# A hand-ordered two-way Mamba scan on one core: scalings of turned states, copies and output products moved in the queues of ScalarE and TensorE

## What is computed

```python
# x: 32 sequences x 256 tokens x 128 channels, fp32
x = x + 0.5 * moe(layernorm(x))                       # 8 experts, 2 per token, hidden 512
x = x + mamba(layernorm(x), w1) + mamba(flip(layernorm(x)), w2)
x = x + 0.5 * moe(layernorm(x))

# mamba: 256 inner channels, 16 states n, depthwise convolution of 4 taps
xi, z = split(x @ in_w.T);  xc = silu(conv(xi) + conv_b)
dt, B, C = split(xc @ xp_w.T);  delta = softplus(dt @ dtp_w.T + dtp_b)
h[n] = h[n] * exp(delta * A[n]) + (delta * xc) * B[n]   # a scan over the 256 tokens
y = sum_n h[n] * C[n] + xc * D;  out = (y * silu(z)) @ out_w.T
```

## Time and profile before

| | before |
|---|---|
| median of 3 runs | 3043.69 us (3041.62 to 3048.03) |
| the profiled execution's own time | 3050.79 us |
| its span | 3048.9 us |
| the Mamba layer's scans, first to last | 653.29 to 2395.38 us |
| busy share: TensorE / VectorE / ScalarE / GpSimd | 84% / 77% / 59% / 74% |

### The profile page before, as it was taken

One profiled execution on the slowest core, in us unless ns is written; L12 is line 12 of the kernel. 1 busy time (PEld: TensorE's weight loads), 2 busy tenths in 40 slices (PEclk: granted clock), 3 DMA queues, 4 the chain that ended last, 5 costly groups with the idle time before them and its releaser, 6 DMA issues.

```text
span 3048.9 us, 41641 instructions
## 1 busy us (share of the span) xinstructions
PE 2546.1 (84%) x12256; PEld 1705.2 (56%) x12256; DVE 2360.4 (77%) x3613; ACT 1809.3 (59%) x3320; POOL 2263.1 (74%) x1360
## 2 busy tenths in 40 slices
PE   4788888868999889989999998998998767888883
PEld 2777778734444444544444444454444457777773
DVE  6755545589999999999999999999998784555556
ACT  3344444457777777777777778777777424444441
POOL 1566656549989899998998989999899535666662
PEclk8899999989999999999999999999999988999997
DMA  6011111143333333333333333333333401111115
GB/s 213 16 40 40 39 38 39 37 155 106 102 94 94 98 95 101 102 94 98 99 98 100 98 97 96 99 102 94 99 99 100 161 12 38 39 39 40 38 40 181
DMA packets 159520, 257.04 MB, mean 84 GB/s; under 512 B 22130, under 2 KB 64018, under 8 KB 158610
## 3 DMA queue, kind: packets, MB, share of 16 engines
q1 hardware_dynamic: 140482, 211.31, 23.4%
q0 software_dynamic: 18464, 37.79, 4.6%
q10 hardware_dynamic: 432, 6.29, 0.5%
HBM read 221.75 MB, written 33.55 MB: 84 GB/s over the span
## 4 chain that ended last, share of the span: by engine, by line
PE 49%; issue 17%; ACT 17%; DVE 10%; POOL 5%; DMA 1%; another core or an unknown queue 1%; SPq 0%; ACTq 0%; POOLq 0%; DVEq 0%
PE bank L1280 14%; PE bank L1446 13%; PE bank L1301 9%; ACT scaled L1142 4%; ACT over L1109 4%; DVE buf L859 4%; POOL buf L493 2%; PE bank L1261 2%; PE bank L1435 2%; POOL buf L506 2%; DVE bank L831 2%; PE bank L1386 2%; DVE X L753 2%; PE bank L1357 2%; ACT bank L1053 1%
## 5 line engine op out<-in xcount | busy, mean ns | idle before, releaser
L506 POOL TENSOR_TENSOR buf<-buf 128x1024 f32<-128x1024 f32 x512 | 1200.8, 2364 | 152.8 <-DVE buf L859 139.4
L1446 PE MATMUL bank<-buf,id_sb 128*128 128x512 f32 x2048 | 977.8, 609 | 46.9 <-ACT bank L1053 39.1
L859 DVE TENSOR_TENSOR_SCAN buf<-over,bank 128x512 f32<-128x512 f32 x768 | 888.2, 1203 | 26.4 <-PE bank L1435 26.4
L1446 PEld LDWEIGHTS bank<-buf,id_sb 128*128 128x128 f32 x2048 | 375.7, 195 | 430.0 <-issue 334.3
L1280 PE MATMUL bank<-parts 128*128 128x256 f32 x3456 | 529.7, 300 | 72.3 <-issue 71.5
L1109 ACT ACTIVATE over<-wgu,negA 128x510 f32<-128x510 f32 x768 | 505.3, 710 | 56.5 <-DVE buf L859 52.7
L455 POOL DMA_INDIRECT token_outputs<-buf,slot_out x288 | 299.1, 1038 | 297.8 <-ACT buf L1004 226.8
L1280 PEld LDWEIGHTS bank<-parts 128*128 128x128 f32 x3456 | 462.8, 200 | 92.3 <-issue 89.5
L725 DVE TENSOR_TENSOR buf<-buf,bank 128x512 f32<-128x512 f32 x288 | 196.8, 684 | 352.1 <-ACT buf L998 205.8
L831 DVE TENSOR_TENSOR bank<-wgu,bank 128x512 f32<-128x512 f32 x512 | 326.9, 684 | 94.8 <-PE bank L1401 62.8
L1301 PE MATMUL bank<-buf 128*128 128x128 f32 x2304 | 307.4, 290 | 92.6 <-issue 67.9
(11 more groups left out here) (166 smaller groups left out, 2839.5 us busy)
## 6 DMA issues: line engine op xcount, KB each, us to landing
buf<-state_rows SPq DMA_DIRECT2D x640, 256.0 KB, 3.3
token_rows<-buf SPq DMA_DIRECT2D x32, 256.0 KB, 2.3
wd_sb<-token_outputs SPq DMA_DIRECT2D x16, 512.0 KB, 4.3
buf<-token_outputs SPq DMA_DIRECT2D x16, 512.0 KB, 5.0
buf<-token_rows,slot_token POOLq DMA_INDIRECT x288
token_outputs<-buf,slot_out POOLq DMA_INDIRECT x288
out<-X SPq DMA_DIRECT2D x16, 256.0 KB, 3.7
wgu<-wgT ACTq DMA_DIRECT2D x1, 2048.0 KB, 8.5
```

Source lines behind the costliest of these rows:

```text
L506: pool.tensor_tensor(hC[:, b, :].rearrange("p (c w) -> p c w", c=C), hs[:, b, :].rearrange("p (c w) -> p c w", c=C), Cs[:, b, :].unsqueeze ...
L859: V.tensor_tensor_scan(hs[:, b, w], dA[:, b, c, :, :].rearrange("p s t -> p (s t)"), source, 0.0, ALU.mult, ALU.add).then_inc(s[f"scan_don ...
L1446: ins = M.matmul(bank[4 + c], id_sb[:, :], hC[:, n % R, c * W:(c + 1) * W], start=False, stop=(n == NS - 1), skip_group_check=True)
```

## The change

- ScalarE scales the turned states 8, 11 and 14 earlier: 8 inside `silus` in state 4 (before: state 6), 11 in state 6 (before: 9), 14 in state 9 (before: 12). State 3 is scaled in state 1 as before.
- ScalarE copies the two halves of duT in states 0 and 1 of the turn (before: state 15 of the turn before, and state 0). In state 9 it copies the columns of B behind the scaling, and the residual copy goes from state 8 to 9, ahead of the scaling.
- TensorE turns the second half of du at the end of its work in state 0; the output product is cut in two halves, in states 7 and 8 (before: whole in 7); and `spread` is issued at another place of the loop.

```diff
-ACT_AT = {"duT0": 15, "duT1": 0, ..., "silus": 4, "xnT": 6, "hi": 7, "res": 8, "BT": 9, ...}
+ACT_AT = {"duT0": 0, "duT1": 1, ..., "silus": 4, "xnT": 6, "hi": 7, "res": 9, "BT": 9, ...}
-SCALE_AT = {1: 3, 6: 8, 9: 11, 12: 14}
+SCALE_AT = {1: 3, 6: 11, 9: 14}
...
-def spread_lead(n):
-    return 1 if on_pool(n - 1) else 2
...
 def silus(p, r, between):            # ScalarE
     for c in range(C):
         act.wait_ge(s["pe_pre"], done(PE_PRE, f"conv{c}_{r}", p))
         step(A.activation(xc[r][:, c * W:(c + 1) * W], bank[6 + c], ACT.Silu, ...))
+    between()                        # scale_by_B of state 8
...
 # ScalarE, in state n
+                        if n == ACT_AT["duT0"]:
+                            copy_duT(p * 2 + r, 0)
                         if n == ACT_AT["duT1"]:
                             copy_duT(p * 2 + r, 1)
...
+                        if n == ACT_AT["res"] and not (first and r == 0):
+                            residual(p * 2 + r - 1, p - 1 if r == 0 else p)
                         if n in SCALE_AT:
                             scale_by_B(p * 2 + r, SCALE_AT[n])
+                        if prep and n == ACT_AT["BT"]:
+                            columns_of_B(2 * pv + rv)
...
 # TensorE, in state n
                         if on_turn(n + 1):
                             turn_back(p, r, n + 1)
-                        for m in (n + 1, n + 2):
-                            if not on_pool(m) and not on_turn(m) and m - spread_lead(m) == n:
-                                ... spread m
+                        m = n + 2
+                        if m < NS and not on_pool(m) and not on_turn(m) and not on_turn(n):
+                            spread(p, r, m)
+                        elif m >= NS and prep and not on_turn(n):
+                            spread(pv, rv, m - NS)
...
-                        if n == PE_AT["duT1"]:      # ahead of the sum and the convolution
-                            turn_du(u, r, 1)
...
+                        if n == PE_AT["duT1"]:      # behind them
+                            turn_du(u, r, 1)
...
-                        if n == PE_AT["out"] and not (first and r == 0):
-                            project_out(u - 1, 1 - r, ...)
+                        if n in (PE_AT["out"], PE_AT["out"] + 1) and not (first and r == 0):
+                            project_out(u - 1, 1 - r, n - PE_AT["out"], ...)
...
+                        if on_turn(n):              # at the end of the state
+                            if n + 2 < NS:
+                                spread(p, r, n + 2)
+                            elif prep:
+                                spread(pv, rv, n + 2 - NS)
```

More of the change, by code:

```diff
@@ L44 @@
 POOL_AT = {"rstd": 0, "du": 12}
-ACT_AT = {"duT0": 15, "duT1": 0, "xn": 2, "skip": 3, "silus": 4, "xnT": 6, "hi": 7, "res": 8, "BT": 9, "parts": 10, "ln": 11}
+ACT_AT = {"duT0": 0, "duT1": 1, "xn": 2, "skip": 3, "silus": 4, "xnT": 6, "hi": 7, "res": 9, "BT": 9, "parts": 10, "ln": 11}
 PE_AT = {"duT1": 0, "z": 4, "xt": 5, "xdbl": 6, "out": 7, "dt": 9, "BT": 9, "duT0": 15}
@@ L816, in gate @@
                 dve.wait_ge(s["y_done"], (u + 1) * NS)
-                wait(dve, s["pe_post"], u)
+                wait(dve, s["pe_post"], 2 * u)
                 for c in range(C):
@@ L1063, in normT, with silus @@
                 A.activation(xnT[:, 1, :, ::-1], src, ACT.Copy).then_inc(s["act_norm"], 1)
-            def silus(p, r):
+            def silus(p, r, between):
                 for c in range(C):
@@ L1097, in residual @@
             def residual(u, p):
-                act.wait_ge(s["pe_post"], u + 1)
+                act.wait_ge(s["pe_post"], 2 * u + 2)
                 A.activation(X[:, p * G:(p + 1) * G, :], bank[7].rearrange("p (t d) -> p t d", t=G),
@@ L1156, in pair @@
                             skip(p * 2 + r, r)
+                        if not prep and n == ACT_AT["silus"]:
+                            scale_by_B(p * 2 + r, TURNED_UNITS[1])
                         if prep and n == ACT_AT["silus"]:
-                            silus(pv, rv)
-                        if prep and n == ACT_AT["BT"]:
-                            columns_of_B(2 * pv + rv)
+                            silus(pv, rv, lambda: scale_by_B(p * 2 + r, TURNED_UNITS[1]))
                         if r == 0 and not last and n == ACT_AT["xnT"]:
@@ L1167, in pair @@
                             decay(pv, rv, n + DECAY_LEAD - NS)
+                        if n == ACT_AT["res"] and not (first and r == 0):
+                            residual(p * 2 + r - 1, p - 1 if r == 0 else p)
                         if n in SCALE_AT:
                             scale_by_B(p * 2 + r, SCALE_AT[n])
-                        if n == ACT_AT["res"] and not (first and r == 0):
-                            residual(p * 2 + r - 1, p - 1 if r == 0 else p)
+                        if prep and n == ACT_AT["BT"]:
+                            columns_of_B(2 * pv + rv)
                         if not prep:
@@ L1186, in _ @@
             normT(0)
-            silus(0, 0)
+            silus(0, 0, lambda: None)
             split_hi(0, 0)
@@ L1193, in _ @@
                 decay(0, 0, n)
-            copy_duT(0, 0)
             pair(0, True, False)
@@ L1377, in project_dt, with project_out @@
                     ins.then_inc(s["pe_pre"], 1)
-            def project_out(u, r, after):
+            def project_out(u, r, half, after):
                 pe.wait_ge(s["gated"], u + 1)
@@ L1383, in project_out @@
                 after()
-                for t in range(G):
+                for t in (2 * half, 2 * half + 1):
                     for c in range(C):
@@ L1490, in pair @@
                                 project_dt(pv, rv)
-                        if n == PE_AT["out"] and not (first and r == 0):
-                            project_out(u - 1, 1 - r, lambda: pe.wait_ge(
+                        if n in (PE_AT["out"], PE_AT["out"] + 1) and not (first and r == 0):
+                            project_out(u - 1, 1 - r, n - PE_AT["out"], lambda: pe.wait_ge(
                                 s["act_pre"], done(ACT_PRE, f"z1_{rv}", pv)) if prep else None)
@@ L1525, in _ @@
                 sum_states(NP - 1, 1, n)
-            project_out(2 * NP - 1, 1, lambda: pe.wait_ge(
-                s["res_done"], 2 * NP - 1))
+            for half in range(2):
+                project_out(2 * NP - 1, 1, half, lambda: pe.wait_ge(
+                    s["res_done"], 2 * NP - 1))
             pe.wait_ge(s["res_done"], 2 * NP)
```

6 lines of the change are left out of this document (removed).

## The result

The changed kernel took 2994.05 us (median of 4 runs, 2991.72 to 2996.36), the kernel before 3042.65 us (4 runs, 3041.55 to 3048.03): a ratio of 0.9837, 95% interval 0.982 to 0.9854, or 49 us less. Between the two profiled executions, from which the sum was made, the span fell from 3048.9 to 2994.4 us, by 54.5. Forecast were 2989 us and 54.5 us. The profiled execution of the kernel before lies 8 us above its median and that of the changed kernel 2 us, so some 6 of the 54.5 us come from which executions were profiled.

The account below looks back on a forecast made before the run. VectorE's 1605 us of work plus 137 us of waits bounds the scans, with TensorE and GpSimd nearly as full. 27.9 + 27.6 + 4 - 5 = 54.5 us off the 3043.7 median gives 2989 us; range 2968 to 3013.

Parts of the forecast that it names:

- TensorE's queue is the path from the gate to product 10: From VectorE's gate to product 10, TensorE's packed queue sets the time, with ScalarE's scaling of 8 as one link.
- Spread rows and halves at 0 us: Moved spread rows keep the same work ahead of them, and halving the output product gains nothing: 0 us.
- Scaling of 8: 27.9 us: TensorE's waits at turn-back 8 go: 1.29 us in fifteen even turns, 0.77 in eleven odd ones; 27.9 us.
- Scaling of 14: 27.6 us: TensorE's 2.39 us wait at turn-back 14 goes, ending VectorE's wait before product 0 (0.20 even, 1.90 odd): 27.6 us.
- I take 27.6 of it: Of VectorE's 29.6 us "issue" waits, 31 times, before product 0, 27.6 us was counted as gain.
- the drop goes with the idle time that led to it: In odd turns TensorE's half-rate clock after its 2.39 us idle, costing two sums 1.7 us more, disappears with that idle.
- GpSimd's times_C of 12 sets product 0, with 0.2 to 0.3 us in hand: At turn's end sum 12 waits for GpSimd's times_C; product 0 is still ready in time, by 0.2 to 0.3 us.
- The rival that GpSimd takes the gain back: GpSimd sets the turn's end; 0.5 us a turn lost at product 0 returns 16 us: 3005 us, 12%.
- The clock still drops: Rival: some eleven clock drops stay in TensorE's packed stretch, returning 19 us: 3008 us, 13%.
- Late copies: 0.3 us in 16 even turns: Later second duT copy on ScalarE makes `skip` late, 0.3 us in 16 even turns: a cost of 5 us.
- Softplus chain: 4 us: ScalarE no longer waits for B's columns before scaling, so pool state 12's decay comes sooner: 4 of 8.7 us.

Follow-up runs that it names:

- the two kernels with rows ahead: Changed kernel with spread row 5 issued ahead of state 3's sum, ratio 0.9792; also row 10 ahead of state 8's sum and half product, 0.9828.
- the second experiment: Kernel before with only the new spread-row place, the output product in halves and the residual copy one state later: 3022.36 us, ratio 1.0001.
- copies back and row 5 ahead: Changed kernel with duT copies as before and spread row 5 issued ahead of the sum of state 3: 2968.33 us, ratio 0.9816.

## Why the prediction held, and where it did not

- *TensorE's queue is the path from the gate to product 10.* Shown: the two kernels with rows ahead only moved the wait down the queue (odd turn 0.8 + 0.5 became 0 + 1.2).
- *Spread rows and halves at 0 us.* Shown by the second experiment.
- *Scaling of 8: 27.9 us.* Alone it brought 29. In the changed kernel the waits before scan 8 fell from 20.6 to 0 us, and those before scan 9 and product 10 went from 34.0 to 22.4 us: 32. I had overestimated what remains at product 10 (1.05 and 0.6; it is 0.7 behind 0.3, and 0.5). One reading was wrong: in turns 1, 3, 5 and 7 TensorE did wait 0.77 us for this scaling, and 1.1 us more behind it for VectorE. In the changed kernel it waits 2.1 us there for VectorE alone, so these turns gave nothing, as I had put it.
- *Scaling of 14: 27.6 us.* It gave 17.3 (29.6 to 12.3 us "issue"). This is the term that was mis-sized. The step that failed is "I take 27.6 of it", which counts the turns 1, 3, 5 and 7 like the others, although the end of the turn had been worked out on turn 15 alone, which has no combine; and with it "the drop goes with the idle time that led to it". In these four turns TensorE had waited 1.68 us at turn-back 14 (2.40 in turn 3); now it waits 2.38 at sum 12, for GpSimd, and the drop comes there. Product 0 waits 2.8 us in each where it had waited 0.95, 1.9, 0.95 and 0.95: 6.3 us more, where I had reckoned with these 4.8 going. In all later turns the waits went as forecast. Alone, the scaling of 14 brought half of its sum, since the drops went to another place.
- *GpSimd's times_C of 12 sets product 0, with 0.2 to 0.3 us in hand.* In the later turns the margin held: no wait. The rival that GpSimd takes the gain back came true in the turns with a combine alone.
- *The clock still drops.* I gave it 13% and eleven drops. In the changed kernel there are four from turn 1 to 7 and none in turns 8 to 30. The profiled execution with copies back and row 5 ahead is this rival in full.
- *Late copies: 0.3 us in 16 even turns.* It is 0.5 in ten of them (10 to 28), and 0 in turns 2 to 8, where a long wait of VectorE at the end of the turn before gives ScalarE the time. The kernel with a quarter of the combine bears that out: ahead of its turns 4 and 6 this wait is 1.1 us instead of 2.8, and product 5 waits 1.3 us in them. With the first turn's 1.4, most of which is a drop of the clock behind `skip` that the changed kernel did not have when it ran again, it makes 7.5 us instead of 5.
- *Softplus chain: 4 us.* 2.9 (9.4 to 6.5), and from the new order, of which the scalings alone show nothing.

32 + 17 + 3 - 7.5 is 45 us, which is what VectorE's waits fell by (1742.1 - 1605.3 = 136.8 to 1692.0 - 1600.1 = 91.9; I had said about 80). VectorE's work fell by 5 besides. It goes with the scalings (1599.7 us with them only, 1605.4 with rows and halves only), but why is open. The last 4 us lie in the expert layers and are chance: all that lies outside the scans took 1277 to 1285 us in the eleven profiles of the experiments, none of which changes it. So the mechanism gave 45 us, 50 with VectorE's work; that the two profiles differ by exactly the forecast 54.5 is luck, and the medians differ by 49.

## What to carry to other kernels

Where an engine in the middle of a chain waits for an operand that has long been computable, put the making of it into an idle stretch of the maker's queue; the gain is the waits in front of a packed queue, not the waits that the last engine shows. Follow the queue row by row before paying for a moved issue: one that has the same work ahead of it moves nothing, and one that is put ahead in a packed queue moves the wait further down. And look at all of TensorE's long waits together: if one is removed while another stays, the clock's drop may only change its place, as it did with the scaling of 14 only and with the combine in state 13, so that two edits that are good alone need not be good together.

## What the hardware showed that I had not expected

**The clock's drop comes behind a long wait of TensorE, and not in every turn.** The waits ahead of a drop to 0.53 to 0.57 were 2.39 us (before, turn-back 14), 2.38 (changed, sum 12 of turn 5), 2.34 (scaling of 14 only, `skip`), 2.24 (copies back and row 5 ahead, `skip`). But the longest wait is not what decides. Waits of 2.39 to 2.41 stood ahead of turn-back 14 in 15 even turns of the kernel before, and the clock dropped at three of them. With row 5 ahead, ten even turns have the same wait for `skip`, 1.65 to 1.88 us, and the clock drops in two of them. Here are TensorE in turn 20 and in turn 22 of that kernel, and for each the busy time by engine ahead of the wait's end and behind it (granted clock 1.00 and 1.00, then 1.00 and 0.50):

```profile
1706.79 1.98 PE L1443 MATMUL bank<-buf,id_sb 128*128 128x512 f32 x4 [1.86 <-ACT bank L1048]
...
1810.80 3.52 PE L1443 MATMUL bank<-buf,id_sb 128*128 128x512 f32 x4 [1.86 <-ACT bank L1048]
```

```profile
1703.40:1706.80 3.40, 1.54 (x5) 0.39 (x3) 3.40 (x5) 3.26 (x7) 3.40 (x3) 1.00 0.46 99
1706.80:1710.20 3.40, 3.40 (x10) 1.68 (x10) 3.40 (x6) 3.37 (x5) 3.40 (x2) 1.00 0.41 103
1807.70:1811.10 3.40, 1.54 (x4) 0.49 (x3) 3.40 (x5) 3.26 (x7) 3.40 (x3) 1.00 0.63 118
1811.10:1814.50 3.40, 3.40 (x5) 1.33 (x4) 2.88 (x5) 3.37 (x6) 3.40 (x2) 0.50 0.31 89
```

The waits of 1.65 to `skip` in the changed kernel's even turns were never followed by a drop; one of 1.66 in turn 30, when that kernel ran again, was. With a drop two sums take 5.4 us instead of the 3.7 of the earlier trace rows. The Trainium skill (TensorE: Matmul & The Clock Gate, Part 1) says that the monitor runs freely beside the program; that fits drops that come in all, in two of ten or in none of like turns.

**VectorE's combine waits for GpSimd's instructions.** The combine (L748) has two inputs in SBUF, while the scans and products of this kernel have one of theirs in PSUM. One of its instructions takes 347 ns as a rule. In state 5 the first of the eight takes 1.49 us: in turn 5 of the changed kernel GpSimd works from 940.29 to 942.65, and the combine's first instruction, begun at 941.30, ends at 942.79. In state 13, where GpSimd has more to do, one took 5.34 us, and turn 5's first took 5.32. The line's durations (minimum, median, maximum in ns) in the kernel with the combine in state 13, then in the changed kernel:

```profile
L748 DVE SCALAR_TENSOR_TENSOR X<-wd_sb,wt,X x128: 320/347/5343, 601.3 to 1085.1; 128x128 f32<-128x128 f32 x128
```

```profile
L748 DVE SCALAR_TENSOR_TENSOR X<-wd_sb,wt,X x128: 320/347/1496, 610.5 to 1053.6; 128x128 f32<-128x128 f32 x128
```

The Trainium skill (SBUF — State Buffer, SBUF: two separate sides) says that VectorE's operations with two SBUF inputs and those of GpSimd that read SBUF share a port pair, that whoever starts first holds it for its whole instruction, and that the other fully blocks. The traces agree: each of the long combine instructions in both kernels ends 0.14 to 0.16 us behind the end of a GpSimd instruction. In the kernel with the combine in state 13 GpSimd works through that of turn 5, which starts at 965.71:

```profile
963.93 2.34 POOL L501 TENSOR_TENSOR buf<-buf 128x1024 f32<-128x1024 f32 x1
966.24 2.34 POOL L520 TENSOR_TENSOR wgu<-wgu 128x1024 f32<-128x1024 f32 x1
968.55 2.34 POOL L501 TENSOR_TENSOR buf<-buf 128x1024 f32<-128x1024 f32 x1
...
975.32 4.68 POOL L501 TENSOR_TENSOR buf<-buf 128x1024 f32<-128x1024 f32 x2 [4.43 <-DVE buf L854]
```

The first combine instruction ends at 971.0, just behind the third row, and the other seven run at their usual rate once GpSimd is idle. So VectorE did not get its turn behind the GpSimd instruction that it found running, but only behind two more. VectorE's busy time in the stretch was 1613.7 us there against 1600.1. That such a wait is shown as busy time is worth knowing: no list of waits names it.
